# Moving the plain fp32 matmuls of a retention block into one stretch per tile, with the retained part on 64x64 quarters

## The chip, the cores and the metric

One NeuronCore of a Trainium2 chip runs the whole kernel. The metric is the device time in microseconds (us) of one execution; less is better. The kernel before takes 426.27 us, the median of three runs (426.12 to 427.16).

## What is computed

One post-norm transformer layer over 4096 tokens (8 sequences of 512, model width 256), all in fp32:

```python
q1, k1 = apply_rotary(x @ Wq, x @ Wk)                  # 4 heads of 64
q, k, v = q1 * 64 ** -0.5, k1, x @ Wv                  # v: 4 heads of 128
gamma = 1.0 - exp2(-5.0 - arange(4))
# retention: o_i = sum over j <= i of gamma^(i-j) (q_i . k_j) v_j
o = rmsnorm(chunk_retention(q, k, v, gamma), gn_weight)
x = layernorm(x + (o * silu(x @ Wg)) @ Wo)
h = silu(x @ w_gate.T / 127) * (x @ w_up.T / 127)      # hidden width 768
x = layernorm(x + h @ w_down.T / 127)
```

## The kernel before

The tokens are cut into 32 tiles of 128. A **slot** `s` is one step of a software pipeline: in slot `s` tile `s` is projected, tile `s - 1` goes through the attention heads, tile `s - 2` through the output projection (`attention_out`), tile `s - 3` is transposed for the feed-forward part (`turn_x1`), gate and up run on pairs of tiles (`FFN_LAG` 4), and tile `s - 6` leaves through the down projection (`down`, `DOWN_LAG` 6). `t` is the tile's place in its sequence, 0 to 3. Slots 0 to 7 (`natural`) hold another layout of the queries and are not the subject. From slot 8 on (`NATURAL`) the queries of a pair of tiles are computed already transposed (`qT`), and every slot does the same work. Slots 12 to 27 are a hardware loop (`Fori`) on every engine; the others are written out. After slot 31 a hand-written `drain` empties the pipeline.

Each engine has its own list, in an order written by hand, and semaphores tie them together. A function of one name exists on several engines: `split_y` is a cast on ScalarE and a subtraction on VectorE. The order on TensorE sets all else. In a steady slot it is: v projection (`project` with `c = 1`), gate and up block 1, down, gate and up block 2 and `keys_and_queries` (in the slots with `t = 1` these two change places), then `recall_and_score` and `update_state`, `turn_x1`, `turn_y`, g projection (`project` with `c = 2`), gate and up block 0 of the next tile, `attention_out`, `retain`, `turn_qk`.

There are two kinds of matmul. The large products are split by hand into high and low parts in the type fp32r (`split_product`, L463; `projection_passes`, L477 and L481). Those on the attention heads and the transposes are **plain fp32**. A plain product is two MATMUL records; a transpose is one. Plain work on the full array: `retain` (L639, four products, heads' masked scores times v, K = 128), `turn_y` (L673), `turn_qk` (L491), `turn_x1` (L628). Plain work on **quarters** of the array (64 rows by 64 columns each, so that four products can run side by side): `recall` (L605, the state of the sequence times q), the scores (L609), the update of the state (L658). A tile with `t = 0` recalls nothing, one with `t = 3` updates nothing.

In this order plain fp32 work comes twice per slot: quarters and transposes between the projections, and `retain` with `turn_qk` behind `attention_out`.

What the steps of the prediction touch: `free_heads` (L567 on) holds the waits ahead of the quarters; `attention_out` waits for `yT_split` and for its bank; `gate_up_block` with `j == 2` waits for `h_ready[0]`, the hidden block 0 that VectorE has multiplied from ScalarE's SiLU. ScalarE's slot is `steady_slot` with `gate`, `gate_v`, `turn_q` (four quarter copies, L895 and L896), `keep_qk`, `copy_v`; VectorE's has `hidden` (L1344), `gated_output` (L1434), `residual_1`, `finish_q` (L1315, L1320), `finish_first_q` (once, in slot 9), `mask`. GpSimd makes the inverse roots and the low parts of h.

Of the kernel before, what the change touches and what calls it, by code (L numbers as in the profile page):

```python
# [35 lines left out]
P = 128  # L36
D = 256
KD = D // P
H = 4
# [40 lines left out]
def build_block(nc, xT, x, w_proj, w_o, gn, w_ffn, rope, rope_by_row, out):  # L80
# [6 lines left out]
    with ExitStack() as ctx:  # L87
# [23 lines left out]
        state = sb("state", [P, 2, DV])  # L111
# [17 lines left out]
        g_sb = sb("g_sb", [P, 2, V])  # L129
# [97 lines left out]
        o_done, state_done = sem("o_done"), sem("state_done")  # L227
        state_half, state_kept = sem("state_half"), sem("state_kept")
# [70 lines left out]

        def q_block(t):  # L300

            return ((t + 1) // 2 % 2, 0) if t % 2 else (t // 2, 1)

        def gate_first(s, t):

            return not natural(s) and t != 1
# [5 lines left out]
        def qk_bank(s, t):  # L312

            return row_bank(t, 0 if natural(s) else 2)

        def v_bank(s, t):

            if not natural(s):
                return row_bank(t, 0)
            return b_ffn[1] if is_slot(s, 0) else row_bank(t, 1 if without_down(s) else 2)  # L320

        def g_bank(s, t):

            return b_ffn[0] if is_slot(s, 0) else row_bank(t, 3)

        def wo_bank(s, t):

            return b_rows[1] if is_slot(s, NT) else b_rows[0] if is_slot(s, NT + 1) else row_bank(t, 4)

        def down_bank(s, t):  # L330
# [3 lines left out]
            return row_bank(t + 1, 1)  # L334
# [99 lines left out]
        def _(pe):  # L434
# [50 lines left out]
            def turn_qk(s, q, t):  # L485

                if exists(s):
                    pe.wait_ge(rotated, s + 1)
                    wait_bank(s, 1, turn_stages)
                    for b in range(0 if natural(s) else 2, 4):  # L490
# [3 lines left out]
            def project(s, q, t, c, done):  # L494
# [21 lines left out]
                elif natural(s):  # L516
                    wait_bank(s, (0, 2, 3)[c], first_row_stages)
                else:
                    wait_bank(s, (2, 0, 3)[c], row_stages)
# [17 lines left out]
                else:  # L537
                    mm = projection_passes(dst, stat, mov, (2, 0, 3)[c] if natural(s) else (None, 2, 3)[c])
# [9 lines left out]
            def keys_and_queries(s, q, t, last_waits=None):  # L548
# [5 lines left out]
                wait_bank(s, 2, row_stages)  # L554
# [12 lines left out]
            def free_heads(s, q, t):  # L567
# [10 lines left out]
                if not natural(n):  # L578
                    pe.wait_ge(q_rotated, s - 8 if tn % 2 else s - 7)
# [10 lines left out]

            def recall_and_score(s, q, t):

                def q_of(n, tn, h):
                    if natural(n):
                        return qkT[half(h), h // 2]
                    return qT[half(h), tn // 2, h // 2, (tn % 2) * P:(tn % 2 + 1) * P]

                n, (qn, tn) = s - 1, back(q, t, 1)
                if exists(n):
                    if natural(s):  # L600
                        free_heads(s, q, t)
                    if tn > 0:
                        for h in range(H):
                            for i in range(2):
                                pe.matmul(o_of(n, h)[half(i)], q_of(n, tn, h)[:, half(i)], state[half(h), h // 2],  # L605
# [1245 lines left out]
```

## Time and profile before

| | |
|---|---|
| median of the runs | 426.27 us (426.12 to 427.16) |
| the profiled execution | 425.66 us |
| its span, first to last instruction | 423.9 us |
| TensorE busy | 418.1 us, 99%, 4311 matmuls |
| TensorE weight loads busy | 396.8 us, 94% |
| VectorE, ScalarE, GpSimd busy | 312.1 (74%), 259.0 (61%), 188.1 us (44%) |
| mean DMA rate | 46 GB/s |
| granted TensorE clock | 1.0 in all 40 slices |

The profile page gives busy times, a chain of work followed back from the last instruction, and groups of instructions by source line. A matmul's record lasts longer (about 280 ns) than the distance to the next one, as matmuls are pipelined and their ends are modelled. What one costs is therefore the distance between the starts of two neighbours, here called the **pitch**.

### The profile page before, as it was taken

Reading aid. Unit: us, or ns where it says so; the run is one execution under the profiler, and the core shown is the slowest. Engines: PE = TensorE matmul, PEld = TensorE weight load, DVE = VectorE, ACT = ScalarE, POOL = GpSimd, SP = SyncE. Lnnn points to the kernel's source line nnn. Section 1 sums busy time; section 2 is a strip of 40 time slices with the busy share of each in tenths; the row PEclk is TensorE's granted clock in tenths of the full one; section 3 lists DMA queues with packets and bytes.
Section 4 is the critical chain, followed back from the end, with each engine's and each line's share of the span. In section 5 each row is a group of like instructions: output and inputs, shape, how many; then the busy total and the mean of one; then the engine's idle time right before and its main releaser. Section 6 shows DMA issues by size and latency. Waiting matters only on the chain.

```text
span 423.9 us, 12406 instructions
## 1 busy us (share of the span) xinstructions
PE 418.1 (99%) x4311; PEld 396.8 (94%) x4311; DVE 312.1 (74%) x907; ACT 259.0 (61%) x796; POOL 188.1 (44%) x330
## 2 busy tenths in 40 slices
PE   8999999999999999999999999999999999999995
PEld 7899999999999999999999999999999999999995
DVE  4999677678676778766777666777766777667785
ACT  6568755577566566566566566565666565565552
POOL 2522343445544344444354444354534354444465
PEclk9999999999999999999999999999999999999999
DMA  8931010201111011110001111011110010100002
GB/s 275 376 120 52 0 53 1 65 2 39 39 40 39 2 40 39 39 37 17 27 31 37 37 37 37 0 37 37 37 37 12 1 40 15 39 14 2 15 27 65
DMA packets 14327, 19.66 MB, mean 46 GB/s; under 512 B 1488, under 2 KB 9808, under 8 KB 14288
## 3 DMA queue, kind: packets, MB, share of 16 engines
q1 hardware_dynamic: 14144, 19.08, 13.8%
q8 instruction: 24, 0.39, 0.4%
q14 instruction: 15, 0.12, 0.1%
q10 hardware_dynamic: 144, 0.07, 0.1%
HBM read 14.94 MB, written 4.19 MB: 45 GB/s over the span
## 4 chain that ended last, share of the span: by engine, by line
PE 97%; DVE 1%; issue 0%; POOL 0%; ACT 0%; POOLq 0%; ACTq 0%; DVEq 0%
PE b_rows L463 29%; PE b_ffn L463 20%; PE b_rows L481 13%; PE b_rows L477 8%; PE b_head L639 7%; PE b_head L609 4%; PE b_turn L673 3%; PE b_head L605 3%; PE b_ffn L628 3%; PE b_turn L491 2%; PE b_state L658 2%; PE b_state L745 1%; DVE wf_int L1367 1%; PE b_rows L524 0%; PE b_ffn L658 0%
## 5 line engine op out<-in xcount | busy, mean ns | idle before, releaser
L1710 POOL TENSOR_TENSOR h_lo<-wf_int,h_hi 128x256 fp32r<-128x256 f32 x96 | 70.9, 740 | 97.3 <-ACT h_hi L1005 97.0
L463 PE MATMUL b_ffn<-x1T_hi,wf_hi 128*128 128x256 f32 x384 | 92.6, 278 | 0.1
L463 PE MATMUL b_ffn<-x1T_lo,wf_hi 128*128 128x256 f32 x384 | 92.1, 277 | 0.0
L463 PEld LDWEIGHTS b_ffn<-x1T_hi,wf_hi 128*128 128x128 f32 x384 | 72.2, 188 | 0.7 <-DVE wf_int L1344 0.5
L463 PEld LDWEIGHTS b_ffn<-x1T_lo,wf_hi 128*128 128x128 f32 x384 | 72.2, 188 | 0.0
L980 ACT ACTIVATE sq<-b_head 128x128 f32<-128x128 f32 x124 | 34.4, 277 | 50.5 <-PE b_head L639 47.5
L1005 ACT CAST h_hi<-wf_int 128x256 fp32r<-128x256 f32 x96 | 38.8, 404 | 40.6 <-DVE wf_int L1344 39.9
L1728 POOL TENSOR_TENSOR ve<-mv,eps 128x1 f32<-128x1 f32 x63 | 13.7, 217 | 87.3 <-DVE mv L1455 71.0
L481 PE MATMUL b_rows<-wp_hi,xT_lo 128*128 128x256 f32 x198 | 50.0, 277 | 0.0
L1344 DVE TENSOR_TENSOR wf_int<-b_ffn,wf_int 128x256 f32<-128x256 f32 x96 | 40.4, 421 | 11.8 <-ACT wf_int L994 9.0
L1446 DVE TENSOR_TENSOR z<-b_rows,x_sb 128x256 f32<-128x256 f32 x32 | 13.6, 425 | 44.7 <-PE b_rows L463 44.7
L994 ACT ACTIVATE wf_int<-b_ffn 128x256 f32<-128x256 f32 x96 | 36.8, 383 | 15.7 <-PE b_ffn L463 13.7
L463 PE MATMUL b_rows<-wf_hi,h_hi 128*128 128x256 f32 x192 | 45.9, 279 | 0.0
L463 PE MATMUL b_rows<-wf_hi,h_lo 128*128 128x256 f32 x192 | 45.6, 277 | 0.0
L1434 DVE SCALAR_TENSOR_TENSOR y<-b_head,rms,g_sb 128x128 f32<-128x128 f32 x124 | 34.9, 345 | 9.7 <-POOL rms L1722 8.7
L481 PE MATMUL b_rows<-wp_hi,xT_hi 128*128 128x256 f32 x138 | 38.4, 278 | 0.0
L481 PE MATMUL b_rows<-wp_lo,xT_hi 128*128 128x256 f32 x138 | 38.2, 277 | 0.0
L1730 POOL TENSOR_TENSOR rs<-ve,half_neg 128x1 f32<-128x1 f32 x63 | 34.3, 544 | 4.9
L481 PEld LDWEIGHTS b_rows<-wp_hi,xT_lo 128*128 128x128 f32 x198 | 35.0, 188 | 1.4
L1722 POOL TENSOR_TENSOR rms<-ms_eps,half_neg 128x4 f32<-128x4 f32 x32 | 35.1, 1097 | 2.5
L463 PEld LDWEIGHTS b_rows<-wf_hi,h_hi 128*128 128x128 f32 x192 | 36.1, 188 | 0.1
L463 PEld LDWEIGHTS b_rows<-wf_hi,h_lo 128*128 128x128 f32 x192 | 36.1, 188 | 0.0
(158 smaller groups left out, 1227.4 us busy)
## 6 DMA issues: line engine op xcount, KB each, us to landing
xT_raw<-in_xT SPq DMA_DIRECT2D x16, 256.0 KB, 2.7
x_sb<-in_x SPq DMA_DIRECT2D x16, 256.0 KB, 2.7
out<-wf_int SPq DMA_DIRECT2D x30, 128.0 KB, 1.7
wf_int<-in_w_ffn SPq DMA_DIRECT2D x6, 384.0 KB, 6.3
wf_int<-in_w_proj SPq DMA_DIRECT2D x6, 256.0 KB, 4.2
rope_sb<-in_rope SPq DMA_DIRECT2D x4, 256.0 KB, 5.7
rope_q<-in_rope_by_row SPq DMA_DIRECT2D x2, 512.0 KB, 8.8
wo_raw<-in_w_o SPq DMA_DIRECT2D x1, 512.0 KB, 6.8
```

The costliest lines, as they stand in the source:

```text
L463: mm = pe.matmul(dst, a, b, start=(i == 0 and j == 0 and not begun), stop=(i == n - 1 and j == len(passes) - 1 and not more), skip_group_c ...
L477: pe.matmul(dst[:], a, b, start=i == 0, stop=False, skip_group_check=True)
L481: mm = pe.matmul(dst[:, cols], a, b[:, cols], start=c == 0 and i == 0, stop=i == n - 1, skip_group_check=True)
L639: mm = pe.matmul(o_of(n, h), attn[:, h, :], v_sb[:, tn % 2, h * DV:(h + 1) * DV], start=False, stop=True, skip_group_check=True)
L980: act.activation(sq[:], o_of(n, h), ACT.Square, scale=float(DV) ** -0.5, accum_out=ms[:, tn % 2, h:h + 1]).then_inc(squared, 1)
L994: act.activation(act_g[:, u], b_ffn[u][:, 0:256], ACT.Silu, scale=SCALE).then_inc(silu_done[j], 1)
L1005: act.copy(h_hi[:, ((t - FFN_LAG) // 2) % 2, hb], h_full[:, u]).then_inc(h_high[j], 1)
L1344: dve.tensor_tensor(h_full[:, u], b_ffn[u][:, 256:512], act_g[:, u], ALU.mult).then_inc(h_ready[j], 1)
L1434: last = dve.scalar_tensor_tensor(y[:, cols], o_of(n, h), rms[:, tn % 2, h:h + 1], g_sb[:, tn % 2, cols], ALU.mult, ALU.mult)
L1710: pool.tensor_tensor(h_lo[:, ring, hb], h_full[:, u], h_hi[:, ring, hb].bitcast(F32), ALU.subtract).then_inc(h_split[j], 1)
L1722: pool.tensor_tensor(rms[:, tn % 2], ms_eps[:, tn % 2], half_neg[:], ALU.pow).then_inc(rms_ready, 1)
L1730: pool.tensor_tensor(rs, ve, half_neg[:, 0:1], ALU.pow).then_inc(rstd, 1)
```

## The change

From slot 9 on (`merged`) a slot has another order on every engine. TensorE's list:

```python
def merged_slot(s, q, t, wide):
    project(s, q, t, 1, v_done)
    keys_and_queries(s, q, t)
    project(s, q, t, 2, g_done)
    gate_up_block(s - 1, q, t - 1, 0, wide)
    gate_up_block(s - 1, q, t - 1, 1, wide)
    attention_out(s, q, t)
    gate_up_block(s - 1, q, t - 1, 2, wide)
    turn_k(s, q, t)
    down(s - 1, q, t - 1, wide)
    stretch(s, q, t)
```

The stretch, with the retained part on quarters. The quarter (j = 1, i = 0) of the masked scores is all zero and is left out, so three of four remain; `crossed` is a semaphore that TensorE waits for on itself:

```python
def retain_quarter(n, tn, h, j, i, start):
    return pe.matmul(o_of(n, h)[half(i)], attn[half(j), h, half(i)],
                     v_sb[half(j), tn % 2, h * DV:(h + 1) * DV], start=start, stop=True, ...)

def retain_crossed(n, tn):
    for h in (0, 2):
        retain_quarter(n, tn, h, 1, 1, h == 0)
        for i in range(2):
            mm = retain_quarter(n, tn, h + 1, 0, i, h == 0)
    mm.then_inc(crossed, 1)

def retain_straight(n, tn):
    pe.wait_ge(crossed, n - NATURAL + 1)
    for h in (0, 2):
        for i in range(2):
            retain_quarter(n, tn, h, 0, i, h == 0 and i == 0)
        mm = retain_quarter(n, tn, h + 1, 1, 1, False)
    return mm

def stretch(s, q, t):
    n, tn = s - 1, back(q, t, 1)[1]
    def heads_and_state():
        pe.wait_ge(masked, n + 1)
        pe.wait_ge(qkT_kept, s + 1)
        pe.wait_ge(q_rotated, s - 7 if t % 2 else s - 6)
        pe.wait_ge(v_copied, s + 1)
        pe.wait_ge(h_ready[1], s - FFN_LAG)
    turn_y(s, q, t, heads_and_state)      # the waits stand before its last transpose
    retain_crossed(n, tn)
    if t < TS - 1:
        quarter_updates(s, t, t).then_inc(state_done, 1)
    mm = retain_straight(n, tn)
    if tn > 0:
        mm = recall(n, tn, True)
    mm.then_inc(o_done, 1)
    scores(s, t, True)
    turn_x1(s, q, t)
```

So the scores and the update of tile `s` are now made in slot `s`, and its retained part in slot `s + 1`. `turn_k` transposes the keys into the free half of `b_state`. Slot 8 is a passage between the two orders: it has the old quarters (recall, scores and update for tile 7), and behind `attention_out` a `first_stretch`:

```python
 def slot(s, q, t, wide):
+    if merged(s):
+        merged_slot(s, q, t, wide)
+        return
     ...
     to_projections(s, q, t, wide)
-    if not is_slot(s, NT - 1):
+    if is_slot(s, NATURAL):
+        attention_out(s, q, t)
+        first_stretch(s, q, t)   # turn_k, retain (full array), scores(8), updates(8)
+    else:
         gate_up_block(s, q, t, 0, wide)
         to_outputs(s, q, t)
```

`attention_out` has lag 3 instead of 2 from slot 9 on, slot 9 has none, and the drain has three. The state has two rings and `g_sb` four. The g projection runs with two passes of 512 columns and four of twice 256 (three and three before). TensorE's loop is written out; the other engines keep theirs:

```python
 def rest(wide):
-    for s in range(FFN_LAG + 1, FIRST_LOOP * TS):
-        slot(s, s // TS, s % TS, wide)
-    with pe.Fori(FIRST_LOOP, NSEQ - 1) as q:
-        for t in range(TS):
-            slot(TS * q + t, q, t, wide)
-    for s in range(NT - TS, NT):
+    for s in range(FFN_LAG + 1, NT):
         slot(s, s // TS, s % TS, wide)
     drain(wide)
```

The lists of ScalarE and VectorE from slot 9 on:

```python
def merged_slot(s, q, t):            # ScalarE
    if not is_slot(s, NATURAL + 1):
        split_x1T(*prev)
    copy_v(s, q, t)
    mean_squares(*prev)
    keep_x1(s, q, t)
    gate_v(s, q, t)
    turn_q(s, q, t, 0)
    gate(s - 1, t - 1, 0)
    turn_q(s, q, t, 1)
    gate(s - 1, t - 1, 1)
    split_h(s - 1, t - 1, 0)
    split_xT(s + 3, ...)
    split_h(s - 1, t - 1, 1)
    keep_k(s)
    gate(s - 1, t - 1, 2)
    split_h(s - 1, t - 1, 2)
    split_y(s, q, t)

def merged_slot(s, q, t):            # VectorE
    split_x1T(*prev); add_lower(s, q, t); add_upper(s, q, t)
    rotate_k(s, q, t); rotate_q(s, q, t); mask(s, q, t)
    moments_2(...); sum_k(s, q, t)
    hidden(s - 1, t - 1, 0); gated_output(*prev); hidden(s - 1, t - 1, 1)
    residual_1(s, q, t); finish_q(s, q, t); moments_1(s - 3, ...)
    hidden(s - 1, t - 1, 2); residual_2(*prev); stats_2(*prev)
    norm_1(s, q, t); split_y(s, q, t); norm_2(*prev)
```

In slot 8 ScalarE runs `turn_q(1)`, `turn_first_q` (four copies), `split_h` of block 2, `keep_k`, `gate_v` in this order, and VectorE's `finish_first_q` follows `finish_q`. The drain is reordered to match: `down` and `attention_out` of the last tiles come between the gate and up blocks, and the last tile's `retain` (full array) and `recall` stand together behind its `turn_y` and `turn_x1`.

## Rows read from the trace of the kernel before

**Rows 1.** The page, part 1: busy us of each engine

```profile
PE 418.1 (99%) x4311; PEld 396.8 (94%) x4311; DVE 312.1 (74%) x907; ACT 259.0 (61%) x796; POOL 188.1 (44%) x330
```

**Rows 2.** The page, part 4: the chain that ended last, by engine

```profile
PE 97%; DVE 1%; issue 0%; POOL 0%; ACT 0%; POOLq 0%; ACTq 0%; DVEq 0%
```

**Rows 3.** Waits of TensorE, whole span: engine line <- releaser: us, times, longest

```profile
PE b_state L745 <- POOL ones L1680: 1.1, 1, 1.1
```

**Rows 4.** Timeline of TensorE, first stretch of a slot: start us, us, what

```profile
203.10 0.28 PE L463 MATMUL b_ffn<-x1T_hi,wf_hi 128*128 128x256 f32 x1
...
203.92 0.28 PE L463 MATMUL b_ffn<-x1T_lo,wf_hi 128*128 128x256 f32 x1
204.13 0.67 PE L609 MATMUL b_head<-qT,qkT 64*64 64x128 f32 x16
204.62 0.28 PE L658 MATMUL b_state<-v_sb,qk 64*64 64x128 f32 x2
...
204.95 0.28 PE L658 MATMUL b_state<-v_sb,qk 64*64 64x128 f32 x2
...
205.17 0.44 PE L628 MATMUL b_ffn<-ident,x 128*128 128x128 f32 x2
205.44 0.60 PE L673 MATMUL b_turn<-ident,y 128*128 128x128 f32 x4
...
206.12 0.39 PE L477 MATMUL b_rows<-wp_lo,xT_hi 128*128 128x512 f32 x1
206.35 0.39 PE L477 MATMUL b_rows<-wp_hi,xT_lo 128*128 128x512 f32 x1
```

**Rows 5.** Timeline of TensorE, second stretch of the same slot

```profile
208.18 0.28 PE L463 MATMUL b_rows<-wo_hi,yT_hi 128*128 128x256 f32 x1
...
209.43 0.28 PE L463 MATMUL b_rows<-wo_hi,yT_lo 128*128 128x256 f32 x1
209.54 1.05 PE L639 MATMUL b_head<-v_sb,attn 128*128 128x128 f32 x8
210.43 0.38 PE L491 MATMUL b_turn<-ident,qk 128*128 128x128 f32 x2
210.57 0.48 PE L477 MATMUL b_rows<-wp_hi,xT_hi 128*128 128x512 f32 x1
```

**Rows 6.** Timeline of TensorE where its loop turns over

```profile
194.55 0.35 PE L463 MATMUL b_ffn<-x1T_hi,wf_hi 128*128 128x256 f32 x1
194.74 0.28 PE L463 MATMUL b_ffn<-x1T_lo,wf_hi 128*128 128x256 f32 x1
```

**Rows 7.** Timeline in the drain: TensorE runs dry behind VectorE

```profile
407.39 0.42 DVE L1391 TENSOR_TENSOR x1T_lo<-b_state,x1T_hi 128x256 fp32r<-128x256 f32 x1
...
407.61 0.28 PE L463 MATMUL b_rows<-wf_hi,h_lo 128*128 128x256 f32 x1
...
407.87 0.38 PE L463 MATMUL b_ffn<-x1T_hi,wf_hi 128*128 128x256 f32 x1
...
408.09 0.28 PE L463 MATMUL b_ffn<-x1T_lo,wf_hi 128*128 128x256 f32 x1
```

**Rows 8.** Timelines of ScalarE and TensorE in slot 8

```profile
92.23 0.36 ACT L896 COPY q_turn<-b_rows 32x256 f32<-32x256 f32 x1
...
93.96 0.41 ACT L895 COPY q_first_turn<-q_first 32x256 f32<-32x256 f32 x1
...
92.44 0.28 PE L463 MATMUL b_ffn<-x1T_hi,wf_hi 128*128 128x256 f32 x1
```

**Rows 9.** Timelines of ScalarE and VectorE in a steady slot

```profile
230.92 0.36 ACT L895 COPY q_turn<-b_rows 32x256 f32<-32x256 f32 x1 [1.46 <-DVE rot_c L1292]
...
233.82 0.60 ACT L959 ACTIVATE g_sb<-b_rows 128x512 f32<-128x512 f32 x1
234.31 0.39 ACT L994 ACTIVATE wf_int<-b_ffn 128x256 f32<-128x256 f32 x1
...
240.01 1.13 DVE L1434 SCALAR_TENSOR_TENSOR y<-b_head,rms,g_sb 128x128 f32<-128x128 f32 x4 [0.46 <-POOL rms L1722]
```

More of the change, by code:

```diff
@@ L589, in free_heads, with q_of, recall, scores @@
                         pe.wait_ge(y_ready, 2)
+            def q_of(n, tn, h):
+                if natural(n):
+                    return qkT[half(h), h // 2]
+                return qT[half(h), tn // 2, h // 2, (tn % 2) * P:(tn % 2 + 1) * P]
+            def recall(n, tn, begun):
+                for h in range(H):
+                    for i in range(2):
+                        mm = pe.matmul(o_of(n, h)[half(i)], q_of(n, tn, h)[:, half(i)],
+                                       state[half(h), ring_of(n, tn - 1), h // 2], start=not begun and h < 2,
+                                       stop=begun, skip_group_check=True)
+                return mm
+            def scores(n, tn, begun):
+                for h in range(H):
+                    for j in range(2):
+                        mm = pe.matmul(scores_of(n, h)[half(j)], qkT[half(h), 2 + h // 2, half(j)],
+                                       q_of(n, tn, h), start=not begun and h < 2, stop=True, skip_group_check=True)
+                mm.then_inc(scores_done, 1)
             def recall_and_score(s, q, t):
[L593 to L596, printed above, removed]
                 n, (qn, tn) = s - 1, back(q, t, 1)
@@ L637, in retain @@
                 pe.wait_ge(v_copied, n + 1)
+                if not begun:
+                    pe.wait_ge(y_ready, n)
                 for h in range(H):
+                    if last_waits and h == H - 1:
+                        last_waits()
                     mm = pe.matmul(o_of(n, h), attn[:, h, :], v_sb[:, tn % 2, h * DV:(h + 1) * DV],
-                                   start=False, stop=True, skip_group_check=True)
+                                   start=not begun and h < 2, stop=not more, skip_group_check=True)
@@ new lines, in retain, with turn_k, last_heads @@
+                if not more:
+                    mm.then_inc(o_done, 1)
+            def turn_k(s, q, t):
+                pe.wait_ge(rotated, s + 1)
+                pe.wait_ge(state_kept, states_to(*back(q, t, 1)))
+                for b in range(2, 4):
+                    mm = pe.transpose(b_state[:, b * P:(b + 1) * P], qk[:, t % 2, b * P:(b + 1) * P], ident[:])
+                mm.then_inc(qkT_done, 1)
+            def last_heads(s, q, t):
+                retain(s, q, t, begun=False, last_waits=lambda: pe.wait_ge(state_kept, 3 * NSEQ), more=True)
+                recall(NT - 1, TS - 1, True).then_inc(o_done, 1)
@@ L1337, in hidden @@
                 dve.wait_ge(silu_done[j], f + 1)
[L1338 removed]
+                if j == 0 and natural(s):
                     dve.wait_ge(z1_stats, s - 1)
```

424 lines of the change are left out of this document (256 added, 168 removed).

## The prediction

> **What bounds the kernel now.** I read the busy times first: TensorE is busy 99% of the span, VectorE 74%, ScalarE 61%, GpSimd 44% [rows 1]. Then the chain that ended last: 97% of it is TensorE [rows 2]. Then the waits of TensorE: one, of 1.1 us, at the very start [rows 3]. So the time is the sum of TensorE's pitches, and an edit is worth what it does to them, as long as the new order leaves TensorE without waits. That second half is the whole question.
>
> What the pitches are: an fp32r pass of 256 columns takes 0.114 us (11 of them between 208.18 and 209.43 [rows 5]), one of 512 columns 0.23 us, a group of four quarter passes 0.11 us (three groups from 204.62 to 204.95 [rows 4]), a plain pass on the full array 0.111 us (8 in 0.89 us [rows 5]).
>
> What is lost between them is seen in the same two groups. Going into the quarters: from 203.92 to 204.62 are 0.70 us, in which one fp32r pass (0.11) and four groups (0.44) lie; 0.15 us is lost. Coming out: from 204.95 to 205.44 are 0.49 us, with one group (0.11) and two transposes (0.22); 0.16 us is lost. Together 0.31 us per slot. The second stretch, plain fp32 on the full array, loses nothing: 209.43 to 209.54 is a normal pitch, the eight passes follow without a gap, and 210.57 comes right behind the transposes [rows 5]. **Plain fp32 itself costs no change-over; only quarters do**, and there was one stretch of quarters per slot already. I put all steps on this reading.
>
> **The change part by part**
>
> *Retained part on quarters.* Four products of two passes on the full array are 8 x 0.111 = 0.89 us. Twelve quarter products of two passes are 24 passes; in `crossed` and in `straight` three different quarters follow each other, so they go three abreast: 8 groups x 0.11 = 0.88 us. Leaving out the zero quarter saves nothing, because the busiest quarter still has eight passes. Gain 0.01 us, in 23 slots 0.2 us.
>
> *One stretch instead of two.* Entries to and exits from the quarters stay at one each per slot. Nothing goes. In a merged slot `turn_k` still stands alone ahead of `down`, but it is full-array work. The two plain-to-fp32r borders of a slot remain two. With the g projection (a 512 pass of 0.23 against two of 0.114, at most 0.01 us) I take 0.2 us for both. Gains so far: 0.4 us (0 to 0.9).
>
> *Slow pitch.* In slots with t = 1 the block before the quarters runs at 0.117 instead of 0.114 us (203.10 to 203.92 [rows 4]): 0.03 us per slot, six slots, 0.2 us, if it goes.
>
> *Loop written out.* Where the loop turns over, one pitch is 0.19 instead of 0.114 us [rows 6]; four turns, the others less: 0.15 us (0.1 to 0.3).
>
> *The new wait inside the stretch.* TensorE waits for its own `crossed`. For t < 3 the four groups of the update (0.44 us) lie between. For t = 3 there is no update, and the wait is bare. A quarter pass is recorded with 0.28 us; a semaphore takes 0.06 us to start TensorE (VectorE ends at 407.39 + 0.42 = 407.81, the next matmul starts at 407.87), and behind an idle TensorE the first pitch is 0.22 instead of 0.11 us [rows 7]. So 0.28 + 0.06 - 0.11 = 0.23 us, up to 0.34 with the slow first pitch; from below 0.15 us, the entry to quarters, which drains the array with no semaphore [rows 4]. I take 0.27 us. Six slots (11, 15 to 31): **1.6 us** (0.9 to 2.0). Queued behind this wait are straight, recall and scores, and behind them all of the next slot.
> What makes the wait necessary is in the Trainium skill, TensorEngine Tiling (Array Packing), Gotcha 1: row tiles may not access one PSUM bank at a time; `crossed` and `straight` exchange rows and banks. No run here shows what comes of leaving it out. It speaks against this change: with the retained part on the full array there is no such border.
>
> *Slot 8.* Its g projection ends where now the gate block starts, at 92.44 [rows 8]. In the new order `attention_out` stands there and its bank waits for `turn_q`, whose last copy ends at 92.23 + 0.36 = 92.59 [rows 8]; before, a gate block of 0.9 us covered this. With 0.06 and the slow first pitch 0.3 us is lost. Then `attention_out` (1.36), `turn_k` (0.22) and three heads (0.67) end at 95.0, and the fourth waits for `keep_k` and the first queries. ScalarE copies four quarters at 0.42 from 92.6 on (the 0.41 us copy of [rows 8]), until 94.3; then VectorE's product and sum, 0.9 us: 95.2. With start-up 0.35 us is lost. And the slot has quarters twice: 0.31 us. Sum **1.0 us** (0.5 to 1.4).
>
> *Slot 9* has no `attention_out`, so gate and up block 2 comes right behind blocks 0 and 1. From its start: v 1.37, keys and queries 1.36, g 1.37, two blocks 1.81: due at 5.9 us. Its `h_ready[0]`: g is out at 4.1 + 0.2, `gate_v` holds ScalarE 0.49 us (233.82 to 234.31), two quarter copies of `turn_q` 0.75, the SiLU 0.39 [rows 9], VectorE's product 0.42 (an operation of this size in [rows 7]) and two semaphores: 6.45 us. Lost, with the slow first pitch: **0.65 us** (0.3 to 0.9).
>
> *Steady slots.* With `attention_out` (1.36 us) in between, block 2 is due at 7.3 us and the same chain has 0.8 us to spare. The next closest is `q_rotated`, which for even t must come from the same slot ahead of the last transpose of `turn_y`, due at 7.28 + 0.91 + 0.22 + 1.36 + 0.33 = 10.1 us. VectorE: `hidden(0)` to 6.35, `gated_output` (four in 1.13 us [rows 9]) to 7.4, `hidden(1)` to 7.75, `residual_1` with its statistics 0.9, `finish_q` 0.9: 9.55 us, 0.5 us ahead. The cost is nothing while this holds. All else (`keep_k`, `y_ready`, `masked`) is over 0.8 us ahead.
>
> *Drain.* The same matmuls and the same number of entries to quarters. Between the last `attention_out` and the last `turn_x1` stand 2.9 instead of 3.2 us of work, and VectorE's chain between them had little to spare: 0.1 us (-0.4 to 0.5).
>
> **The sum.** 1.6 + 1.0 + 0.65 + 0.1 - 0.4 - 0.2 - 0.15 = +2.6 us. Against the profiled execution of 425.66 us that is 428.3 us. The median of the runs stands 0.6 us above that execution, so 428.9 us. About 1.3 us (0.3%) is what a measurement of this kernel can tell from no change.
>
> **The rivals**
>
> *A, a chain becomes the bound (slower still).* `q_rotated` comes late in the even slots. It decides once VectorE's chain is over 0.5 us longer than I add it up, for instance by ScalarE being late with its SiLU. For: seven operations in a row, each with a semaphore, and VectorE at 74% [rows 1]. Against: it was never late before. At 0.3 us each, 11 slots (10 to 30): +3.3 us, 432.2 us. Chance 0.13.
>
> *B, the new waits cost next to nothing (no change).* The bare wait costs little more than a pitch, and slots 8 and 9 are half as late as I add up: 428.9 - 1.6 - 1.0 = 426.3 us. For: the prices come from records whose ends are modelled. Against: the two semaphore chains of slot 8 and 9 are simple sums. Chance 0.25.
>
> *C, faster.* The entry to the quarters costs 0.15 us behind an fp32r pass; no row shows it behind a plain fp32 pass, which is where the new order puts it. If it were free there, 24 x 0.15 = 3.5 us go; with B's wait: 428.9 - 3.5 - 1.6 = 423.8 us. For: one border less between kinds of work. Against: both kinds have records of about 0.28 us, so the array has as much to finish. Chance 0.12.
>
> *D, the quarters don't run three abreast.* If products kept strict order, the second pass of each would hold up the next one: 13 groups instead of 8, 0.55 us per slot, 12.6 us in all, 441.5 us. Against: the update's groups hold four products of different quarters within 0.11 us though each has two passes [rows 4]. Chance 0.04.
> The Trainium skill (TensorE: Matmul & The Clock Gate, Part 3) says that matmuls start and end in program order, which is what D would need; the trace of this kernel shows side by side what such an order would have drawn apart.
>
> **How the numbers follow.** The forecast has 0.46, A 0.13, B 0.25, C 0.12, D 0.04. The forecast's own range is 427.2 to 430.7 us, about 0.07 of it within 0.3%. Slower by over 0.3%: 0.39 + 0.13 + 0.04 = 0.56. Within: 0.07 + 0.25 = 0.32. Faster: 0.12. The range leaves out C and D and reaches from B's lower side to A's near side: 425.6 to 431.9 us.
>
> **What would show it.** In the changed profile: in slots with t = 3 a gap of about 0.27 us between two groups of the retained part, none for t < 3; one gap ahead of `attention_out` and one in the fourth head in slot 8; one of some 0.6 us ahead of block 2 in slot 9; 0.3 us per slot for entry and exit as before; eight groups per tile of the retained part; no wait in the steady slots. Wrong would be: a TensorE that idles before the last transpose of `turn_y`, an entry to the quarters that is cheaper than 0.15 us, or a retained part under 0.88 us.

## The result: slower, by more than forecast

| | before | after |
|---|---|---|
| median of the runs | 426.72 us (426.12 to 427.62) | 433.67 us (432.26 to 434.33) |
| ratio | | 1.015 (95% interval 1.0131 to 1.0168) |
| the profiled execution, its span | 425.66 us, 423.9 us | 434.33 us, 432.5 us |
| last matmul ends at | 419.31 us | 426.08 us |

The forecast was 428.9 us, at most 431.9. The direction was right, the size was not: 7 us instead of 2.6. Almost all of it is on TensorE: its last matmul ends 6.8 us later. What follows it (norm, last store) took 1.8 us longer in this profiled execution; among the profiled executions of kernels with the same code there it took 4.6 to 6.5 us, and the medians stand 6.95 us apart. So I explain the 6.8 us and not the rest.

The page after, part 1 (busy us of each engine) and the first line of part 4 (the chain), against [rows 1, 2]:

```profile
PE 423.4 (98%) x4702; PEld 400.1 (93%) x4702; DVE 315.3 (73%) x907; ACT 263.4 (61%) x796; POOL 182.9 (42%) x330
PE 96%; DMA 1%; ACT 0%; issue 0%; DVE 0%; SPq 0%; ACTq 0%
```

TensorE is still what bounds the kernel, and it has hardly become idler. The waits of its matmuls after (engine, tile and line <- releaser: us, times, longest) are these. The first is that of [rows 3], the second lies at the start of the program, the third is slot 9, where the forecast had put one:

```profile
PE b_state L863 <- POOL ones L1853: 1.1, 1, 1.1
PE b_rows L539 <- ACT wp_hi L1152: 0.5, 2, 0.3
PE b_ffn L472 <- DVE wf_int L1489: 0.4, 1, 0.4
```

So the greater part of the loss is not in waits. It has to be in the pitches, and there it is. Lines have moved: 463 is 472 now, 477 is 486, 481 is 490. The timeline of TensorE after (start us, us, what), from the last pass of the query block to `down` of one slot, is this (`...` marks lines left out):

```profile
202.78 0.28 PE L472 MATMUL b_rows<-xT_hi,wp_lo 128*128 128x256 f32 x1
202.90 0.39 PE L486 MATMUL b_rows<-wp_hi,xT_hi 128*128 128x512 f32 x1
203.13 0.39 PE L486 MATMUL b_rows<-wp_lo,xT_hi 128*128 128x512 f32 x1
203.36 0.28 PE L490 MATMUL b_rows<-wp_hi,xT_lo 128*128 128x256 f32 x1
203.47 0.28 PE L490 MATMUL b_rows<-wp_hi,xT_hi 128*128 128x256 f32 x1
...
208.54 0.38 PE L680 MATMUL b_state<-ident,qk 128*128 128x128 f32 x2
208.68 0.37 PE L472 MATMUL b_rows<-wf_hi,h_hi 128*128 128x256 f32 x1
208.88 0.28 PE L472 MATMUL b_rows<-wf_hi,h_lo 128*128 128x256 f32 x1
...
210.14 0.60 PE L785 MATMUL b_turn<-ident,y 128*128 128x128 f32 x4
```

From 203.36 to 208.54 lie 44 pitches in 5.18 us: 0.1178 us each. From 208.88 to 210.14, in `down` of the same slot, 11 pitches take 1.26 us: 0.115 (the first three and the last are 0.116 to 0.120, the seven between 0.1133 in the mean). The granted clock is 1.0 in both stretches, and TensorE is busy without a hole in both; one view by windows (us, busy us, matmuls, granted clock, DMA share, GB/s) says so:

```profile
203.36:208.54 5.18, 5.18 (x45) 1.00 0.01 3
208.88:210.14 1.26, 1.26 (x13) 1.00 0.00 0
```

The usual pitch is 0.1133 us, the long one 0.1178: 4.5 ns or 4% more. It is the 0.117 us of 203.10 to 203.92 in [rows 4], where it lasted for seven passes in one slot out of four. After the change it lasts from g to `turn_k`, over g, all three gate and up blocks and `attention_out`, in every slot from 10 on. Counted over the whole trace (runs of at least four pitches of 116 to 125 ns, each behind a pass of 256 columns or a transpose) there are 208 long ones before and 1123 after: 915 x 4.5 ns = **4.1 us**.

The quarters are as forecast. The same timeline in the merged stretch:

```profile
210.14 0.60 PE L785 MATMUL b_turn<-ident,y 128*128 128x128 f32 x4
210.67 0.55 PE L690 MATMUL b_head<-v_sb,attn 64*64 64x128 f32 x9
210.96 0.32 PE L765 MATMUL b_ffn<-v_sb,qk 64*64 64x128 f32 x1
211.05 0.28 PE L690 MATMUL b_head<-v_sb,attn 64*64 64x128 f32 x3
...
211.59 0.50 PE L690 MATMUL b_head<-v_sb,attn 64*64 64x128 f32 x9
...
212.57 0.44 PE L655 MATMUL b_ffn<-ident,x 128*128 128x128 f32 x2
212.76 0.48 PE L486 MATMUL b_rows<-wp_hi,xT_hi 128*128 128x512 f32 x1
```

The last of four transposes starts at 210.47 (210.14 and three pitches of 0.11), the first quarter at 210.67: the entry costs 0.09 us there, and the second group starts 0.160 us behind the first instead of 0.109, 0.05 more. That is 0.14 us together, the same as the 0.15 of [rows 4]. Nine passes, then three more make `crossed`, and the first pass of the update slips in at 210.96 ahead of the last `crossed` group at 211.05. In slots with t < 3 there is no gap.

### The profile page after: what moved, and what is told of

It is laid out like the page before. It is cut to its first block, busy times and chain, and to the rows that moved or that the text cites. A ratio compares the mean times of both kernels' runs of the same rounds, so it can differ in the third digit from the quotient of the medians.

```text
span 432.5 us, 13142 instructions
## 1 busy us (share of the span) xinstructions
PE 423.4 (98%) x4702; PEld 400.1 (93%) x4702; DVE 315.3 (73%) x907; ACT 263.4 (61%) x796; POOL 182.9 (42%) x330
## 4 chain that ended last, share of the span: by engine, by line
PE 96%; DMA 1%; ACT 0%; issue 0%; DVE 0%; SPq 0%; ACTq 0%
PE b_rows L472 30%; PE b_ffn L472 21%; PE b_rows L490 14%; PE b_rows L486 6%; PE b_head L690 5%; PE b_head L628 4%; PE b_turn L785 3%; PE b_head L619 2%; PE b_ffn L655 2%; PE b_ffn L765 2%; PE b_head L670 2%; PE b_state L680 1%; DMA wf_int<-in_w_proj 1%; PE b_turn L500 1%; PE b_state L765 1%
## 5 line engine op out<-in xcount | busy, mean ns | idle before, releaser
L1893 POOL TENSOR_TENSOR ms_eps<-ms,eps 128x4 f32<-128x4 f32 x32 | 7.2, 225 | 130.2 <-ACT sq L1108 130.1
L490 PE MATMUL b_rows<-wp_hi,xT_lo 128*128 128x256 f32 x244 | 59.3, 278 | 0.0
L472 PE MATMUL b_rows<-wf_hi,h_hi 128*128 128x256 f32 x192 | 48.3, 290 | 0.0
L490 PEld LDWEIGHTS b_rows<-wp_hi,xT_lo 128*128 128x128 f32 x244 | 42.2, 189 | 2.3
L1076 ACT CAST x1T_hi<-b_ffn 128x256 fp32r<-128x256 f32 x29 | 10.8, 374 | 49.6 <-PE b_ffn L655 49.6
L472 PE MATMUL b_rows<-wo_hi,yT_hi 128*128 128x256 f32 x128 | 36.2, 283 | 0.1
L472 PE MATMUL b_rows<-wo_lo,yT_hi 128*128 128x256 f32 x128 | 35.8, 280 | 0.0
```

What stands on the lines that cost most here:

```text
L472: mm = pe.matmul(dst, a, b, start=(i == 0 and j == 0 and not begun), stop=(i == n - 1 and j == len(passes) - 1 and not more), skip_group_c ...
L490: mm = pe.matmul(dst[:, cols], a, b[:, cols], start=c == 0 and i == 0, stop=i == n - 1, skip_group_check=True)
```

## The experiments

The first four runs below "after" in the table were made on one chip, the next four on a second and the last four on a third. The kernel before, run beside them, took 427.8, 427.3 and 427.4 us. The runs below that give no interval were executed once, so for them the trace and the period count and not the time. "Four-slot period" is the distance between the same transposes of `turn_y` sixteen slots apart, divided by four. It is 51.105 us before and 51.953 after. It is taken from one trace of each kernel, whose steady slots repeat to some 10 ns. "Long pitches" are counted as above.

| run | time, us | period, us | long pitches |
|---|---|---|---|
| before | 426.72 | 51.105 | 208 |
| after | 433.67 | 51.953 | 1123 |
| g in narrow passes | 434.93 | 52.147 | 1349 |
| queries first | 430.63 | 51.490 | 525 |
| retained part on the full array | 432.92 | 51.773 | 1109 |
| before, gate block behind the queries | 427.19 | 51.146 | 305 |
| g's wide passes last | 435.41 | 52.153 | 1361 |
| query passes in another order | 434.02 | 51.967 | 1092 |
| x^T moved by 64 bytes | 434.66 | 51.877 | 820, and more in shorter runs |
| three edits together | 431.06 | 51.287 | 416 |
| pass between, weights loaded | 436.28 | 52.444 | 1112 |
| pass between, x^T loaded | 433.77 | 51.873 | 426 |
| low part of x^T moved | 433.16 | 51.953 | 1158 |
| before, loop written out | 427.37 | 51.159 | 225 |

### Which part starts the long pitch

*g in narrow passes.* In the changed kernel the g projection has no 512-column passes:

```diff
-(None, 2, 2 if merged(s) else 3)[c]
+(None, 2, 0 if merged(s) else 3)[c]
```

> The changed kernel with the g projection in passes of 256 columns only (from slot 9 on; before: two of 512 and eight of 256). The changed kernel runs the 44 fp32r passes from the g projection to turn_k at a pitch of 0.118 us instead of 0.113 us in 23 slots. Theory W (passes of 512 columns behind passes of 256 start the slow pitch): it disappears, 44 x 23 x 0.0045 = 4.5 us less, about 429.2 us. Theory Q (whatever stands behind the query block runs slow): it stays and begins with the first pass of g; 433.7 to 434 us.

Measured: 434.93 us (ratio to before 1.0171, 1.011 to 1.0231), and the long pitch begins at the first pass of g, 48 of them in a slot. The wide passes don't start it. What comes right ahead is the query block.

*Queries first.* The query block ahead of the key block in the merged slots; nothing else moves:

```diff
+if merged(s) and has_q(s, t):
+    query_block(dst, *q_block(t))
+    split_product(dst[:, 256:512], stat, mov).then_inc(qk_done, 1)
+    return
```

> The changed kernel with the queries ahead of the keys, so that the g projection stands behind the keys' passes (x as weights, Wk streaming) and not behind the query block (Wq as weights, x streaming). Theory Q: the slow pitch goes or moves to the keys only, about 4.5 us less, 429.2 us. Theory W: nothing changes, 433.7 us; the slow pitch still begins behind the two wide passes of g.

Measured: 430.63 us (1.0065, 1.004 to 1.0091), period 51.490. The long pitch moves with the query block. Its timeline, from the end of the queries over the keys into g:

```profile
202.61 0.28 PE L472 MATMUL b_rows<-xT_hi,wp_lo 128*128 128x256 f32 x1
202.72 0.28 PE L472 MATMUL b_rows<-wp_hi,xT_hi 128*128 128x256 f32 x1
...
203.43 0.40 PE L486 MATMUL b_rows<-wp_hi,xT_hi 128*128 128x512 f32 x1
203.67 0.40 PE L486 MATMUL b_rows<-wp_lo,xT_hi 128*128 128x512 f32 x1
203.90 0.28 PE L490 MATMUL b_rows<-wp_hi,xT_lo 128*128 128x256 f32 x1
204.02 0.28 PE L490 MATMUL b_rows<-wp_hi,xT_hi 128*128 128x256 f32 x1
```

Six key passes take 0.71 us (0.118 each), the two wide ones 0.235 each, and then it is over: 0.113 again up to `turn_k`. Between the queries and the keys stands no wait and no semaphore here, so neither is the cause. The period falls by 0.46 us, 2.5 us over 22 slots; 598 fewer long pitches are 2.7 us. The 4.5 us that were expected did not come: 525 long ones are left, of which six in a slot are the keys' and 4 to 11 more in each slot are in `down`. There the long pitch begins behind the two transposes of `turn_k` (209.23 to 210.41 are ten pitches of 0.118), while in the kernel after, which arrives at `turn_k` with long pitches, it ends there.

*Before, gate block behind the queries.* The kernel before, with its third gate and up block behind the keys and queries in every slot, as it was in slots with t = 1 alone. All else is untouched:

```diff
-return not natural(s) and t != 1
+return False
```

> The kernel before with the order of its slots with t = 1 in all slots: keys_and_queries, then gate and up block 2, then the quarters. Theory Q: block 2 runs at 0.118 us in every slot from 8 on, 18 more slots x 8 passes x 0.0045 = 0.65 us more, 427.3 us. Theory W: no 512-column passes are moved, so no slow pitch is added; 426.6 us. No wait of TensorE in either.

Measured: from slot 8 on every slot has seven long pitches in that block, where one slot out of four had them. The old order is as prone to it as the new one; it only had the plain fp32 work right behind the queries, which ends the long pitch before it lasts. The period grew by 0.041 us, where three slots with seven long pitches more would be 0.095. The difference is that this run has none of the odd pitches as that of [rows 6] (0.14 us over the loop) and none of the 23 long ones that stand behind them before: over sixteen slots 61 long pitches more and 0.14 us less are 0.13 us, 0.034 for four. The time of the one execution, 427.19 us, says nothing either way.

### Whether wide passes end it

I had read "queries first" as: two passes of 512 columns, met at the long pitch, end it. So I put g's two wide passes at its end:

```diff
-for i in range(whole):            # passes 1 and 2, 512 columns, first
+for i in range(n - whole, n):     # passes 5 and 6, 512 columns, last
```

> The changed kernel (433.7 us) with one edit: the g projection of slots 9 to 31 takes its two passes of 512 columns at its end (passes 5 and 6 of both halves) instead of at its beginning (passes 1 and 2). Theory P, the long pitch (0.118 instead of 0.113 us) is a state that the end of the query block starts and that two passes of 512 columns met in that state end: the 8 passes of 256 columns at the head of g run at 0.118, the two wide ones at 0.236, and everything behind them up to turn_k at 0.113; of 44 long pitches in a slot 8 stay, 22 slots x 36 x 0.0045 = 3.6 us go: 430.1 us. Theory R, it is tied to what the passes behind the query block read (they would be long in whatever order): 48 long pitches in a slot, 434 us. Theory S, the two wide passes start the state: they would hand it on to gate and up again, from there to turn_k 34 long pitches in a slot and none in g: 432.7 us.

Measured: 435.41 us (1.0199, 1.0176 to 1.0222), 8 long pitches in g, the wide passes at 0.23, and 36 more behind them, up to `turn_k`; and 11 behind `turn_k` in `down`. None of my three theories gave that: the long pitch was started by the query block, as P had it, but the wide passes did not end it. There are 1361 long ones in all, and the time goes with the count: 238 more than after, 1.1 us, and the period is 0.200 us longer, 1.1 us over 22 slots.

### What at the end of the query block does it

*Query passes in another order*, so that another pair of operands comes last:

```diff
-(sh, mh), (sh, ml), (sl, mh)
+(sl, mh), (sh, mh), (sh, ml)      # query block only
```

> The changed kernel with one edit: the three passes of each half of the query block in another order (low part of the weights first, then high by high, then the low part of x^T streamed last, instead of high by high, low part of x^T, low part of the weights), in slots 9 to 31 and in the slots ahead of them. Theory T, the last pass of the block and what stands beside it in memory start the long pitch: with another last pair the long pitches from g to turn_k (44 in a slot) go and the four-slot period falls from 51.95 to about 51.2 us, the whole to about 429.7 us. Theory P, the state is started by the change from streamed x^T to streamed weights, whichever pair comes last: still 44 in a slot and 433.7 us.

Measured: 434.02 us, still 44 long pitches in a slot. Which pass is last doesn't matter.

*x^T moved by 64 bytes.*

```diff
+sb("shift_x", [P, LINE])
 xT_hi = sb("xT_hi", [P, 2, KD, 2 * P], F32R)
 xT_lo = sb("xT_lo", [P, 2, KD, 2 * P], F32R)
+sb("shift_back", [P, 512 - LINE])
```

> The changed kernel with x^T (both parts) placed 64 bytes further in each partition, all tiles behind it placed 2048 bytes further; nothing else. Theory A, the long pitch comes from where x^T lies against the weights that are loaded beside it: the 44 long pitches in a slot change their place or their number (none: 429.7 us; or they begin inside the query block itself). Theory P, it doesn't matter where x^T lies: 44 in a slot, from g to turn_k, and 433.7 us.

Measured: 434.66 us, period 51.877, and a wholly different picture. The timeline of this run, from the keys and queries over g into the gate block:

```profile
203.04 0.27 PE L474 MATMUL b_rows<-xT_hi,wp_lo 128*128 128x256 f32 x1
...
203.97 0.28 PE L492 MATMUL b_rows<-wp_hi,xT_lo 128*128 128x256 f32 x1
...
204.93 0.28 PE L474 MATMUL b_ffn<-x1T_hi,wf_hi 128*128 128x256 f32 x1
...
205.16 0.28 PE L474 MATMUL b_ffn<-x1T_hi,wf_hi 128*128 128x256 f32 x1
...
205.95 0.28 PE L474 MATMUL b_ffn<-x1T_lo,wf_hi 128*128 128x256 f32 x1
```

The passes with x^T in them are nearly all long now, in v, keys, queries and g (8 pitches from 203.97 to 204.93: 0.119 each; the twelve of keys and queries 0.1187, where the kernel after has 0.1134), and the gate block runs at 0.113 from its third pass on (7 pitches from 205.16 to 205.95). The edit moves x^T by 64 bytes and all that lies behind it by 2048. So **where an operand begins in its partition changes the pitch**, which theory P had denied, and at this place of x^T the long pitch no longer outlives the passes that cause it. The sum of both is about the same time.

*A pass between.* That led to theory B: in the unmoved kernel x^T, the feed-forward weights, y^T and h begin 64 bytes past a multiple of 512, the projection weights, wo and x1^T at a multiple, and only at the end of the query block is an operand loaded from the same offset as the one that is streamed. One pass more between queries and g removes that meeting, or, with the other stationary operand, keeps it:

```diff
+if merged(s) and c == 2 and has_q(s, t):
+    pe.matmul(dst[:, 0:256], wp_hi[:, 0, 0, 0:P], wp_hi[:, 0, 0, 256:512], start=True, stop=True)
```

> The changed kernel with one pass more in each of slots 9 to 31, between the query block and g: 128x128 of the query weights as the stationary operand, 256 columns of the same weights streamed, into g's bank, whose first own pass clears it. In the partitions x^T, the feed-forward weights, y^T and h begin 64 bytes past a multiple of 512, the projection weights, wo and x1^T at a multiple of 512. Everywhere the operand that is loaded lies 64 bytes (or 192 the other way) from the one that is streamed meanwhile; only where the query block ends, x^T (64) is streamed while x^T (64) is loaded for g. Theory B, that one meeting starts the long pitch: with the added pass the weights (0) are loaded beside x^T (64), and x^T (64) beside the weights (0), so no meeting is left and the 44 long pitches in a slot go: 433.7 + 22 x 0.113 - 22 x 44 x 0.0045 = 431.9 us, the four-slot period 51.95 + 0.45 - 0.79 = 51.61. Theory P, the change from streamed x^T to streamed weights starts it: 45 long pitches, the first on the added pass, 436.3 us, period 52.42.

> The control to the run with a pass between: the same added pass at the same place, but with x^T (high part, 64 bytes past a multiple of 512) as its stationary operand, so that x^T is still loaded while x^T is streamed. Theory B: the meeting is back, the long pitch from the added pass on up to turn_k, 44 or 45 in a slot, 433.7 + 2.6 = 436.3 us, four-slot period 52.42. If the added pass cures by being there (one pass more between two chains of sums), it would do so here too: 431.9 us, 51.61.

Measured: the opposite. Without the meeting, 436.28 us (1.0216, 1.0175 to 1.0257), period 52.444, and 44 long pitches in a slot behind it. With it, 433.77 us, period 51.873: the added pass costs its 0.113 us and yet the period is *shorter* than after. The timeline of the second:

```profile
202.85 0.28 PE L472 MATMUL b_rows<-xT_hi,wp_lo 128*128 128x256 f32 x1
202.96 0.28 PE L537 MATMUL b_rows<-wp_hi,xT_hi 128*128 128x256 f32 x1
203.08 0.40 PE L486 MATMUL b_rows<-wp_hi,xT_hi 128*128 128x512 f32 x1
203.31 0.39 PE L486 MATMUL b_rows<-wp_lo,xT_hi 128*128 128x512 f32 x1
203.55 0.28 PE L490 MATMUL b_rows<-wp_hi,xT_lo 128*128 128x256 f32 x1
203.67 0.28 PE L490 MATMUL b_rows<-wp_hi,xT_hi 128*128 128x256 f32 x1
```

The added pass (line 537) has the long pitch, two wide ones follow at 0.235, and by 203.67 it is over, as in "queries first", and as there `down` is long instead, 11 pitches in every slot. Theory B is refuted. What both cures have in common is one or more long passes of x^T against the projection weights, then g's two wide passes, then narrow passes of g. Wide passes right behind the queries (after), behind a pass with loaded weights, or behind g's own narrow passes (wide last) do not do it. Why this sequence ends the long pitch stays open.

*Low part of x^T moved*, on top of the other order of query passes, as the last test of an offset:

```diff
+sb("shift_lo", [P, 4 * LINE])
 xT_lo = sb("xT_lo", [P, 2, KD, 2 * P], F32R)
+sb("shift_back", [P, 512 - 4 * LINE])
```

> The kernel with the query block's passes in the other order (low part of x^T streamed last; 434.0 us, 44 long pitches in a slot) with one edit more: the low part of x^T begins 320 bytes past a multiple of 512 instead of 64, all tiles behind it 2048 bytes further. Where the query block ends, x^T low (320) is then streamed while x^T high (64) is loaded. Theory B with a distance counted in 512 bytes: no meeting, the 44 long pitches go, 429.7 us, period 51.2. Theory B with a distance counted in 256 bytes: 320 and 64 are the same, 44 stay, 434 us. If the new distances between x^T low and the projection weights (320) are bad ones themselves, long pitches show inside g, the keys and the queries, as in the run with x^T moved by 64 bytes.

Measured: 433.16 us, 44 long pitches in a slot, period 51.953, equal to after. 256 bytes more change nothing here, where 64 bytes of both parts had changed all. By itself this would fit an offset counted in 256 bytes, but theory B is out already.

### The other terms

*Retained part on the full array*, without `crossed`, in the merged slots:

```diff
-retain_crossed(n, tn)
+for h in range(H):
+    mm = pe.matmul(o_of(n, h), attn[:, h, :], v_sb[:, tn % 2, h * DV:(h + 1) * DV],
+                   start=h < 2, stop=True, skip_group_check=True)
```

> The changed kernel with the retained part on the full array (4 products of two passes) between turn_y and the quarters, so without the wait for crossed. The bare wait cost 0.31 us in each of six slots (1.9 us in all); the full array costs 0.016 us more per slot (0.4 us). Theory: 1.5 us less, 432.2 us, no gap in slots with t = 3. Rival (the gap is the border between two users of one bank and not the wait): a gap of about that size stays in front of the first quarters, no change, 433.7 us.

Measured: 432.92 us (1.013, 1.007 to 1.0191), period 51.773, 0.18 us less than after. The wait at t = 3 is gone. What it had cost, in the waits of the weight loads of after:

```profile
PEld b_head L690 <- PE b_head L690: 1.9, 6, 0.3
```

Six waits, as forecast, of 0.31 us each. What one of them adds to the time is seen in the length of the stretch, from `turn_y` to `turn_x1`. Slots with t = 0 and with t = 3 hold the same number of groups in it (sixteen: the update in the one, the recall in the other), but t = 0 has no bare wait. The stretch shown above, t = 0, lasts from 210.14 to 212.57, 2.43 us. Slot 31, t = 3, in the kernel after and then in this run:

```profile
391.42 0.60 PE L785 MATMUL b_turn<-ident,y 128*128 128x128 f32 x4
...
394.15 0.33 PE L655 MATMUL b_ffn<-ident,x 128*128 128x128 f32 x1
```

```profile
390.77 0.60 PE L786 MATMUL b_turn<-ident,y 128*128 128x128 f32 x4
...
393.23 0.44 PE L655 MATMUL b_ffn<-ident,x 128*128 128x128 f32 x2
```

That is 2.73 us against 2.43: the bare wait costs **0.30 us**, 0.25 ahead of the next group and 0.05 ahead of the one behind it, as at an entry to the quarters; six of them are 1.8 us. On the full array the stretch takes 2.46 us in both kinds of slot, 0.027 more than the quarters without the wait (by the starts to the ns). So the quarters gain 0.027 us in a slot, 0.6 us over 23 slots, and lose 1.8 by their wait. For four slots 0.30 - 4 x 0.027 = 0.19 us, and the period shows 0.18.

*Before, loop written out.* The kernel before with TensorE's loop over four slots written out, which is all that this edit does:

```diff
-with pe.Fori(FIRST_LOOP, NSEQ - 1) as q:
-    for t in range(TS):
-        slot(TS * q + t, q, t, wide)
-for s in range(NT - TS, NT):
+for s in range(FFN_LAG + 1, NT):
```

> The kernel before with TensorE's loop over four slots written out and nothing else. My forecast took 0.15 us for it: the pitches of 0.19 us where the loop turns (194.55 to 194.74) become 0.113 three or four times. So 427.6 us against 427.75 beside it, not to be told from no change; the trace should show those pitches gone. A rival: fetching more code costs pitches elsewhere, and the time rises by 0.5 us or more.

Measured: 427.37 us against 427.39 (ratio 0.9998, 0.9977 to 1.0018). No change, as expected, but for a reason that I had not: the odd pitch does not belong to the loop's turn. It is still there, at the same place of the same slot. The timeline:

```profile
196.16 0.35 PE L463 MATMUL b_ffn<-x1T_hi,wf_hi 128*128 128x256 f32 x1
196.35 0.28 PE L463 MATMUL b_ffn<-x1T_lo,wf_hi 128*128 128x256 f32 x1
```

That is [rows 6] again, 1.6 us later, as this execution started its steady part 1.6 us later. In the changed kernel there is no such pitch. So the part of the expectation that these pitches would be gone did not come true. What makes them stays open, but they aren't harmless: the passes behind this one have the long pitch, 19 of them in this run as in the kernel before. This run also has 41 long pitches in a row from 302.40 on, behind plain fp32 work and two wide passes of v, at a place where the kernel before has only the last seven of them, though the two issue the same matmuls in the same order. So the block ahead isn't the only thing that decides; what else does stays open.

*Three edits together*: queries first, the full array, and in slot 9 `down` ahead of the third gate and up block.

```diff
+if is_slot(s, NATURAL + 1):
+    down(s - 1, q, t - 1, wide)
+    gate_up_block(s - 1, q, t - 1, 2, wide)
+    turn_k(s, q, t)
```

> What the runs so far point to, put together: in slots 9 to 31 the query block stands ahead of the key block (worth 3.0 us alone), the retained part runs on the full array again without its wait (worth 0.75 us alone), and in slot 9 down stands ahead of the third gate and up block, so that the block's wait of 0.70 us is over by then. If the three add up: 433.7 - 3.0 - 0.75 - 0.7 = 429.2 us, still 1.5 us above the kernel before taken beside it (427.7): slot 8 costs 1.0 us and the six slow passes of the keys in each slot 0.6. If down finds its own parts late in slot 9, the 0.7 us is paid there: 429.9 us. If the passage at slots 8 and 9 is hidden and not on the path, it would be at the time of before, 427.5 to 428.

Measured: 431.06 us (1.0098, 1.0075 to 1.0121), 1.9 us over the sum. The period, 51.287, is what the first two give (51.490 - 0.18 = 51.31). The third edit failed, and cost about as much again as it was to save, which is 1.4 of the 1.9 us. TensorE in slot 9, first the changed kernel, then this one:

```profile
102.86 0.28 PE L472 MATMUL b_ffn<-x1T_lo,wf_hi 128*128 128x256 f32 x1
103.56 0.39 PE L472 MATMUL b_ffn<-x1T_hi,wf_hi 128*128 128x256 f32 x1 [0.42 <-DVE wf_int L1489]
103.79 0.28 PE L472 MATMUL b_ffn<-x1T_lo,wf_hi 128*128 128x256 f32 x1
```

```profile
102.69 0.28 PE L472 MATMUL b_ffn<-x1T_lo,wf_hi 128*128 128x256 f32 x1
103.76 0.39 PE L472 MATMUL b_rows<-wf_hi,h_hi 128*128 128x256 f32 x1 [0.80 <-ACT q_turn L1032]
103.99 0.28 PE L472 MATMUL b_rows<-wf_hi,h_lo 128*128 128x256 f32 x1
```

`down` waits longer than the block did, for a bank: the slot's keys and queries lie in it until ScalarE's quarter copies (`q_turn`) are done. Both orders wait for ScalarE's chain in that slot; 102.69 to 103.99 are two pitches, so `down` loses 1.07 us where the block lost 0.70, and a transpose of `turn_y` later in the slot loses another 0.34. I had looked at what `down` reads and not at where it writes. No kernel of these beats the one before.

## Why the prediction was wrong

What the last matmul's 6.8 us consist of, against the terms of the sum:

| term | forecast, us | measured, us |
|---|---|---|
| long ("slow") pitch | -0.2 | +4.1 |
| bare wait for `crossed`, six slots | +1.6 | +1.8 |
| slot 8 | +1.0 | +1.0 |
| slot 9 | +0.65 | +0.7 |
| drain, retained part, borders, start: the rest | -0.3 | -0.7, as what is left over; the retained part is -0.6 of it (forecast -0.2) |
| loop written out | -0.15 | -0.14, but not by the loop |

- **The step that failed is "Slow pitch".** It held the right number, 0.117 instead of 0.114 us behind 203.10 [rows 4], and took it for a trait of the block that stood there in slots with t = 1. So it was to go when that block moved. It goes with what stands *ahead*, the query block, and in the steady slots it lasts until the next plain fp32 work, be it only the two transposes of `turn_k`. The change sets the query block 44 fp32r passes (and two wide ones) ahead of the next plain work, in every slot, where before the quarters followed at once in three slots of four. "Queries first" and the gate block behind the queries in the kernel before show this; in numbers, 915 x 4.5 ns are +4.1 us where the term had -0.2. These 4.3 us are all that the forecast lacked; its other terms are off by 0.2, 0.05 and -0.4 us, and that these nearly cancel is luck. Why the query block starts the long pitch stays open. The rows for it were there: the long pitch began directly behind the queries in the one kind of slot where fp32r passes followed them, and else in the steady slots only behind two odd pitches (19 behind that of [rows 6], and four).
- **"Plain fp32 itself costs no change-over; only quarters do"** was right as it stood, entry and exit cost 0.3 us per slot as before, and I put all steps on it. It is not the whole truth: the pitch of what follows can change at plain fp32 work. In the kernel before, the quarters right behind the queries ended the long pitch before it cost anything. But plain work isn't a sure end of it. In "queries first" `turn_k` starts it, and near the end of the kernel before it begins right behind the eight passes of `retain`, with 23 long pitches:

```profile
385.72 1.05 PE L639 MATMUL b_head<-v_sb,attn 128*128 128x128 f32 x8
...
386.72 0.28 PE L463 MATMUL b_rows<-wo_lo,yT_hi 128*128 128x256 f32 x1
386.84 0.28 PE L463 MATMUL b_rows<-wo_hi,yT_lo 128*128 128x256 f32 x1
```

- **The bare wait** was 0.30 us where 0.27 was taken (up to 0.34 was allowed), in the six slots named.
- **The retained part** gained 0.027 us a slot where 0.01 was taken: its eight groups of 0.109 us are 0.87 us, against eight passes of 0.111 to 0.112.
- **Slot 8**: 0.38 us at the first passes of `attention_out`, 0.28 in the fourth head, 0.31 for the second stretch of quarters: 0.97 us, forecast 0.3 + 0.35 + 0.31. The rows for the first:

```profile
92.47 0.28 PE L490 MATMUL b_rows<-wp_hi,xT_lo 128*128 128x256 f32 x1
92.88 0.36 PE L472 MATMUL b_rows<-wo_hi,yT_hi 128*128 128x256 f32 x1
93.08 0.28 PE L472 MATMUL b_rows<-wo_lo,yT_hi 128*128 128x256 f32 x1
```

- **Slot 9**: 102.86 to 103.56 and on to 103.79 are 0.93 us for two pitches, 0.7 lost, forecast 0.65.
- **Steady slots**: no wait of any engine ahead of the last transpose of `turn_y`. Rival A, a late `q_rotated`, did not happen.
- **Rival C**, a free entry from plain fp32, is refuted: 0.14 us of entry remain. **Rival D**: the quarters do go three abreast; 12 groups of `crossed`, update and `straight` start between 210.67 and 211.92.
- **Rival B** priced the new waits at next to nothing; they cost what the forecast had them at. Its own sum has a slip: half of slots 8 and 9 is 0.8 us and not 1.0, which makes it 426.5 us.
- **The loop** was costed at the right size from the wrong cause, so that this term came out is luck.

The range failed with its step. It was built of errors of the waits and of rivals in the waits. Nothing in it let the pitch itself move, though TensorE makes some 4,000 pitches and 0.0045 us on a quarter of them (1123) is 5 us, more than all the new waits together.

## What to carry to other kernels

When an engine is busy 99% of the span, an edit that only reorders can still cost a per cent through the distance between instructions: measure the pitch of equal passes in every part of a slot before, and ask of each deviation what stands ahead of it and what ended it. Before moving work apart, list what follows each block in the old order, as the pitch of a block can depend on the block ahead of it. And for work moved ahead, look at the bank that it writes as well as at the data that it reads.

## What the runs showed of the hardware

- An fp32r pass of 256 columns against 128x128 weights has two pitches that last, at the same granted clock of 1.0: 0.1133 and 0.1178 us (0.226 and 0.235 for 512 columns). The record of the weight load starts 3 to 5 ns behind the matmul of the pass before it either way; the matmul starts 0.110 us behind its own load in the one case and 0.114 to 0.115 in the other. The long pitch persists over passes with other operands and other banks.
- It started behind a block with x^T streamed against the projection weights, independent of a semaphore there, of which pass is last and of the passes behind it. It also started in some places, not in all, behind idle time (34 long ones in the drain of the kernel before, none that last behind the idle of slots 8 and 9 after), behind an odd pitch as that of [rows 6], behind the two transposes of `turn_k` (4 to 11 in `down`) and behind eight plain passes on the full array (23). In the steady slots after, it ended at the two transposes of `turn_k` (44 long pitches ahead of them, in six slots of 22 another 4 behind them). In two runs it ended behind some long passes of x^T, then two of 512 columns, and then narrow ones.
- Where an operand lies matters. x^T 64 bytes further (and what lies behind it 2048), the passes with x^T of one slot were at 0.112 to 0.123 us, 0.119 in the mean, while the gate block ran at 0.113 from its third pass on. The Trainium skill (TensorE: Matmul & The Clock Gate, Part 2, Step-by-step) says that loading the next weights takes no SBUF read bandwidth from the running matmul. The traces don't settle it: with nothing changed but places in SBUF, the twelve pitches of keys and queries took 0.1187 instead of 0.1134 us each, so the place counts for something. That load and stream disturb each other would explain it, but is my reading and not shown; what the rule of offsets is stays open, and the one that I tried (equal offsets meet) is refuted.
- A bare wait of TensorE for its own last group of quarter passes costs 0.30 us; going from a transpose into the quarters costs 0.14 us and coming out 0.16.
- Quarter passes of different products are not bound to the order of the program: at 210.96 the first pass of the update starts ahead of the last `crossed` passes at 211.05, which are issued ahead of it.
- From one profiled execution to another the steady part began up to 1.7 us earlier or later, and the end behind the last matmul took 4.6 to 6.5 us. Differences of a few tenths were read from the period for that reason.
